# In the first attention, VectorE forms the difference of the two softmax maps and GpSimd normalises the head outputs

## The chip, the cores and the metric

The kernel runs on one core of one Trainium2 chip. The metric is the time of one launch in microseconds (us) on the device; the kernel before takes 1631.5 us, the median of three runs (1629.63 to 1633.35). Inside a core five engines run their own instruction queues and meet at semaphores: TensorE (PE, and PEld for its weight loads), VectorE (DVE), ScalarE (ACT), GpSimd (POOL) and SyncE (SP), which issues most transfers.

## The reference, cut to what matters

The program is two transformer blocks on a batch of 2 sequences of 1024 rows and 256 columns. The change lies in the attention of the first block, a differential attention: each of 8 heads has two causal softmax maps, and the second is subtracted with a factor.

```python
p1 = attn_map(q[:, :, :, 0], k[:, :, :, 0])
p2 = attn_map(q[:, :, :, 1], k[:, :, :, 1])
lam = lam1 - lam2 + LAMBDA_INIT
p = p1 - lam * p2
o = jnp.einsum('bhqk,bkhe->bqhe', p, v)
rms = jax.lax.rsqrt(jnp.mean(o * o, axis=-1, keepdims=True) + EPS)
o = o * rms * subln_w
o = o * (1.0 - LAMBDA_INIT)
return o.reshape(B, S, H * D) @ out_w.T + out_b
```

After it come a gated feed-forward layer with a Hadamard transform, a second attention with 16 small heads, and a feed-forward layer with a shared part and eight routed experts. None of these is touched.

## The kernel before, in words

**Groups and steps.** The 8 heads of the first attention are worked in 4 groups of 2 heads per sequence, `attn0_group(b, g, out, last)`. The heads of a group share their keys and values. A group has 16 steps: steps 0 to 7 are the eight query tiles (128 rows) of the first head, steps 8 to 15 those of the second. Step n has i + 1 key tiles of 128 columns for query tile i, so its width goes from 128 to 1024 columns in steps 0 to 7 and again in 8 to 15. In the last group of a sequence the second head takes its tiles in the order 0, 1, 2, 3, 5, 7, 6, 4. Groups 1 and 2 of a sequence are one loop on the device; groups 0 and 3 are written out.

**One step.** TensorE multiplies queries and keys into two PSUM tensors, one for each map (`scores`, three passes of split float32). VectorE takes each row's negated maximum (`nmax`, L1806). ScalarE takes the exponential into E1 and E2 with the row sums in `lsum` (L1407). VectorE takes the reciprocals `rsum` (L1772) and forms `mixc` (L1774), which is minus lambda times sum 1 over sum 2. GpSimd multiplies E2 with `mixc` (L2271) and adds E1 (L2274); so E1 holds the difference up to the factor 1 / sum 1. TensorE turns E1 (`transpose_p`, L916), ScalarE rounds the result to PT_h (L1389), VectorE keeps the rest in PT_l (L1781), TensorE multiplies with the values (`weigh_values`), and VectorE evicts to O with the factor `rsum` (L1786).

**Who waits for whom.** The work of several steps is laid in one another. In step s VectorE has, in this order: `mix(s - 1)`, `low(s - 2)` (PT_l), the two maxima of step s, the eviction of a value tile with its bias (L1810, steps 0 to 5), and `output(s - 3)`. ScalarE has `high(s - 2)` (PT_h), the two exponentials of step s, the rounding of value tiles to V_h (L1411, steps 0 to 5) and the sum of squares of an output tile (L1394). TensorE has `transpose_p(s - 2)`, `scores(s)`, `weigh_values(s - 3)`. There is one PSUM tensor for each map, so `scores(s)` of a map waits until the exponential of step s - 1 has read it (semaphore `exp_done`). E1 and E2 are double buffered.

**GpSimd beside it.** In its queue, behind the two instructions of each step, stand V_l (the low part of a value tile, L2250: two each in steps 0 and 1, one each in steps 2 to 5), the low part of the next group's weights Wa_l (one piece each in steps 8 to 11), and at the end of a group the scaling of Wo_raw (L2262) and Wo_l.

**The out product.** A group's outputs are normalised and multiplied with the output weights while the next group runs (`out` is true for groups 1 to 3). VectorE normalises tile t of both heads into `On[t % 2]` with the factors `orstd` (L1724, two instructions of 256 columns): tiles 0 and 1 in steps 2 and 3, tiles 2 to 7 behind the low parts of the turned tiles 1 to 6, in steps 8 to 11. TensorE turns `On` (L844) in steps 7 to 11, ScalarE and VectorE split it (L1365, L1731), TensorE multiplies, and VectorE adds to X (L1767). The last group of a sequence has nothing behind it; its outputs are normalised by VectorE (tiles 0 and 1) and GpSimd (tiles 2 to 7, L2308) in its tail. Under "tail" the text means what stands behind step 15 (`tail0`).

Of the kernel before, what the change touches and what calls it, by code (L numbers as in the profile page):

```python
# [30 lines left out]
ALU = mybir.AluOpType  # L31
AX = mybir.AxisListType

P = 128
B, T, HID = 2, 1024, 256
NT = T // P
# [12 lines left out]
UNITS0 = 12  # L49
SPLIT_STEPS = (8, 9, 10, 11)  # L50
STEPS0 = 2 * NT

# [42 lines left out]
def program(nc, d, ctx):  # L95
# [203 lines left out]
    mix_ready = sem("mix_ready")  # L299
    mix_scaled = sem("mix_scaled")  # L300
    p_ready = sem("p_ready")
# [1346 lines left out]
    def _(dve):  # L1648
# [70 lines left out]
        def out_normalise(it, g, t):  # L1719

            if t >= 2:
                dve.wait_ge(ot_ps, NT * it + t - 1)
            for h in range(2):
                ins = nc.vector.tensor_scalar(On[t % 2][:, h:h + 1, :], O[:, t, bass.ds(g % 2 * 2 + h, 1), :],  # L1724
                                              orstd[:, h * NT + t:h * NT + t + 1], None, ALU.mult)
            ins.then_inc(on_done, 1)
# [29 lines left out]
        def attn0_group(b, g, out, last):  # L1756
            it = b * GROUPS0 + g

            def project_out(s, late):
                for kind, t in out0(s, late) if out else ():  # L1760
                    if kind == "t":
                        out_low(it - 1, t)
                        if 1 <= t < NT - 1:
                            out_normalise(it - 1, g + 1, t + 1)
                    else:
# [4 lines left out]
            def mix(n):  # L1770
# [4 lines left out]
                                               scalar=lsum[:, n % 4, 0:1], in1=neglam[:], op0=ALU.mult,  # L1775
                                               op1=ALU.mult).then_inc(mix_ready, 1)

            def low(n):
# [11 lines left out]
            for s in range(STEPS0):  # L1790
                if s >= 1:
                    mix(s - 1)
                if out and s in (2, 3):
                    if s == 2 and last:
                        dve.wait_ge(xb_done, 2 * b + 1)
                    elif s == 2:
                        dve.wait_ge(xd_in, 16 * b + 16)
                    out_normalise(it - 1, g + 1, s - 2)
                if s >= 2:
# [448 lines left out]
    def _(pool):  # L2248
# [14 lines left out]

        def attn0_group(b, g, last):
            it = b * GROUPS0 + g
            for n in range(STEPS0):
                w = (q_tile(n, last) + 1) * P
                e1, e2 = E1[n % 2][:, 0:w], E2[n % 2][:, 0:w]
                pool.wait_ge(mix_ready, STEPS0 * it + n + 1)
                pool.nop(nofuse=True)  # L2270
                nc.gpsimd.tensor_scalar(e2, e2, mixc[:, n % 4:n % 4 + 1], 1.0, ALU.mult,  # L2271
                                        ALU.mult).then_inc(mix_scaled, 1)
                pool.wait_ge(mix_scaled, STEPS0 * it + n + 1)
                nc.gpsimd.tensor_tensor(e1, e1, e2, ALU.add).then_inc(p_ready, 1)  # L2274
                for t in v_tiles(n):
                    pool.wait_ge(v_hi, NT * it + t + 1)
                    low(V_l[:, t, :].unsqueeze(1), O[:, t, bass.ds(g % 2 * 2 + 1, 1), :],
                        V_h[:, t, :].unsqueeze(1)).then_inc(v_lo, 1)
                if n in SPLIT_STEPS:
                    split_wa(it + 1, SPLIT_STEPS.index(n))  # L2280
                if last and n == STEPS0 - 2:
                    scale_wo(it)
# [14 lines left out]

        def out_normalise(b, t):

# [12 lines left out]
        def attn0_out(b):  # L2312
            for t in range(2, NT):
                out_normalise(b, t)
            ffn_split(b, 0)
# [29 lines left out]
        for b in range(B):  # L2345
            attn0_group(b, 0, False)
            with pool.Fori(1, GROUPS0 - 1) as g:
                attn0_group(b, g, False)
            if b == 0:
                pool.wait_ge(const_in, CONSTS * 16)  # L2350
            pool.wait_ge(y_added, 3 * NT * b + (GROUPS0 - 2) * NT)
            add_bias(0)
            attn0_group(b, GROUPS0 - 1, True)
            attn0_out(b)
# [127 lines left out]
```

## Time and profile before

| | before |
|---|---|
| time, median of three runs | 1631.5 us |
| span of the profiled execution | 1649.7 us |
| PE busy | 1550.0 us (94%) |
| DVE busy | 1101.0 us (67%) |
| ACT busy | 930.4 us (56%) |
| POOL busy | 636.6 us (39%) |
| one group of the first attention with an out product | 106.3 us |

The span is that of one execution under the profiler, from its first to its last instruction; the page gives no time outside the span. The span is 18.2 us above the median of the runs. The eight groups of the first attention lie from about 29 to 430 us (first sequence) and from about 844 to 1246 us (second). A row of the chain or of the waits names the instruction that waited, what it waited for, and for how long.

### The profile page before, as it was taken

How to read it: one execution, taken by the hardware profiler on the slowest of the kernel's cores; microseconds unless marked ns; L12 is line 12 of the kernel's file. 1: busy time of each engine (PE TensorE's matmuls, PEld its weight loads, DVE VectorE, ACT ScalarE, POOL GpSimd, SP SyncE). 2: the span in 40 equal slices, each digit the busy share in tenths (PEclk: the TensorE clock that was granted, in tenths of full speed). 3: DMA queues.
4: the chain of work that ended last, by engine and by line, in shares of the span. 5: the costliest groups of instructions: out<-in, count | busy, mean ns of one | idle time of the engine just before them, and what ended most of it. 6: DMA issues, size and time to landing. Idle time of an engine off the chain costs nothing.

```text
span 1649.7 us, 30985 instructions
## 1 busy us (share of the span) xinstructions
PE 1550.0 (94%) x10774; PEld 1341.8 (81%) x10774; DVE 1101.0 (67%) x2705; ACT 930.4 (56%) x2054; POOL 636.6 (39%) x582
## 2 busy tenths in 40 slices
PE   8999999999899999999898999999998999998985
PEld 7888889888888677688787898898988876776885
DVE  6767667677645787574577676676766377874655
ACT  5666565665444577543556655656654346775353
POOL 1635444554461101252535354444654510031631
PEclk9999999999999999999999999999999999999998
DMA  3110000020120422034220200000201113322132
GB/s 132 46 52 17 27 1 16 25 91 1 40 69 10 75 51 61 21 120 137 76 96 1 77 18 26 16 7 18 91 1 58 50 36 61 60 60 101 56 126 106
DMA packets 48195, 88.03 MB, mean 53 GB/s; under 512 B 9600, under 2 KB 30480, under 8 KB 46928
## 3 DMA queue, kind: packets, MB, share of 16 engines
q1 hardware_dynamic: 43552, 75.28, 15.9%
q0 software_dynamic: 3744, 10.26, 1.7%
q8 instruction: 77, 1.26, 0.3%
q10 hardware_dynamic: 768, 0.79, 0.2%
q14 instruction: 54, 0.44, 0.1%
HBM read 60.18 MB, written 19.76 MB: 48 GB/s over the span
## 4 chain that ended last, share of the span: by engine, by line
PE 66%; DVE 15%; ACT 9%; issue 6%; POOL 3%; ACTq 1%; DMA 0%; DVEq 0%; POOLq 0%; SPq 0%
PE ps L408 16%; PE ps L410 15%; PE ps L409 15%; PE ps L1193 4%; PE ps L1210 4%; PE ps L1153 4%; ACT E L1407 3%; DVE nmax L1806 3%; PE ps L916 2%; POOL E L2274 2%; ACT PT_h L1389 1%; DVE On L1724 1%; DVE PT_l L1781 1%; PE ps L1189 1%; PE ps L844 1%
## 5 line engine op out<-in xcount | busy, mean ns | idle before, releaser
L1407 ACT ACTIVATE E<-ps,nmax 128x128 f32<-128x128 f32 (+7 forms) x256 | 188.9, 741 | 208.5 <-DVE nmax L1806 208.2
L2271 POOL TENSOR_SCALAR E<-E,mixc 128x128 f32<-128x128 f32 (+7 forms) x128 | 97.0, 758 | 396.2 <-DVE mixc L1774 396.2
L1806 DVE TENSOR_REDUCE nmax<-ps 128x1 f32<-128x128 f32 (+7 forms) x256 | 183.3, 749 | 12.7 <-PE ps L893 12.5
L1568 ACT ACTIVATE PT<-ps 128x512 f32<-128x512 f32 x288 | 155.0, 601 | 58.8 <-PE ps L1193 57.7
L2274 POOL TENSOR_TENSOR E<-E 128x128 f32<-128x128 f32 (+7 forms) x128 | 182.4, 1425 | 10.7
L408 PE MATMUL ps<-V_h,PT_h 128*128 128x256 f32 x576 | 168.0, 292 | 0.5 <-DVE O L1786 0.5
L409 PE MATMUL ps<-V_l,PT_h 128*128 128x256 f32 x576 | 163.8, 284 | 0.0
L410 PE MATMUL ps<-V_h,PT_l 128*128 128x256 f32 x576 | 163.6, 284 | 0.0
L408 PE MATMUL ps<-K_h,Q_h 128*128 128x512 f32 (+3 forms) x384 | 147.4, 384 | 8.7 <-ACT E L1407 5.4
L2026 DVE CUSTOM_DVE_ANT_0 masked<-ps,causal 128x128 bf16<-128x128 f32 (+3 forms) x256 | 111.1, 487 | 39.5 <-PE ps L1153 37.8
L1781 DVE TENSOR_TENSOR PT_l<-ps,PT_h 128x128 fp32r<-128x128 f32 (+7 forms) x128 | 96.7, 756 | 60.7 <-ACT PT_h L1389 60.0
L410 PE MATMUL ps<-K_h,Q_l 128*128 128x512 f32 (+3 forms) x384 | 133.2, 347 | 0.0
L409 PE MATMUL ps<-K_l,Q_h 128*128 128x512 f32 (+3 forms) x384 | 132.7, 346 | 0.0
L1153 PE MATMUL ps<-KS,QS 128*128 128x512 f32 (+3 forms) x384 | 111.9, 371 | 3.3 <-issue 1.4
L408 PEld LDWEIGHTS ps<-V_h,PT_h 128*128 128x128 f32 x576 | 110.5, 192 | 2.2 <-issue 0.9
L1193 PE MATMUL ps<-QS,KS 128*128 128x512 f32 (+3 forms) x384 | 112.2, 361 | 0.0
L409 PEld LDWEIGHTS ps<-V_l,PT_h 128*128 128x128 f32 x576 | 110.8, 192 | 0.5
L410 PEld LDWEIGHTS ps<-V_h,PT_l 128*128 128x128 f32 x576 | 110.6, 192 | 0.0
L408 PE MATMUL ps<-XT_h,Fw_h 128*128 128x512 f32 x256 | 102.6, 401 | 5.9 <-DVE XT_l L1654 2.8
L1866 DVE TENSOR_TENSOR Hf<-ps,silu_g 128x512 f32<-128x512 f32 x64 | 44.2, 691 | 88.8 <-PE ps L410 74.0
L916 PE MATMUL ps<-ident,E 128*128 128x128 f32 x576 | 85.0, 275 | 19.1 <-POOL E L2274 18.8
L409 PE MATMUL ps<-XT_l,Fw_h 128*128 128x512 f32 x256 | 100.9, 394 | 1.1 <-issue 1.0
(265 smaller groups left out, 4622.8 us busy)
## 6 DMA issues: line engine op xcount, KB each, us to landing
Wa_raw<-in_wa SPq DMA_DIRECT2D x8, 1024.0 KB, 6.0
Fw_raw<-in_fa SPq DMA_DIRECT2D x32, 256.0 KB, 2.6
E_raw<-in_fe SPq DMA_DIRECT2D x8, 768.0 KB, 7.5
xs<-in_xs SPq DMA_DIRECT2D x2, 2967.0 KB, 12.6
Wo_raw<-in_wo SPq DMA_DIRECT2D x8, 512.0 KB, 3.5
yg<-ys SPq DMA_DIRECT2D x8, 512.0 KB, 5.2
xg<-xs SPq DMA_DIRECT2D x6, 645.0 KB, 8.1
KS<-QK_h SPq DMA_DIRECT2D x56, 64.0 KB
```

Of the source, the lines that this page charges most:

```text
L408: nc.tensor.matmul(out, a_h, b_h, start=start, stop=False, **kw)
L409: nc.tensor.matmul(out, a_h, b_l, start=False, stop=False, **kw)
L410: return nc.tensor.matmul(out, a_l, b_h, start=False, stop=stop, **kw)
L916: mm = nc.tensor.transpose(ps[2][:, tile(kb)], E1[n % 2][:, tile(kb)], ident[:])
L1153: mm = nc.tensor.matmul(bank1(j % RING1)[:, at:at + z - a], QS[:, 2 * (p % Q_PAIRS) + n, tile(i)], KS[:, p % K_PAIRS, a:z], start=at == 0, ...
L1193: mm = nc.tensor.matmul(bank[:, at:at + z - a], KS[:, p % K_PAIRS, tile(kb)], QS[:, 2 * (p % Q_PAIRS) + n, a:z], start=not diagonal and k ...
L1407: nc.scalar.activation(e[:, 0:w], ps[m][:, 0:w], ACT.Exp, bias=nmax[:, s % 4, m:m + 1], accum_out=lsum[:, s % 4, m:m + 1]).then_inc(exp_do ...
L1568: nc.scalar.activation(PT[:, at:at + HALF], bank1(RING1 + n % RING1), ACT.Exp, scale=SCALE1).then_inc(t_used, 1)
L1781: nc.vector.tensor_tensor(PT_l[n % 2][:, 0:w], ps[2][:, 0:w], PT_h[n % 2][:, 0:w].bitcast(F32), ALU.subtract).then_inc(pt_lo, 1)
L1806: nc.vector.tensor_reduce(nmax[:, s % 4, m:m + 1], ps[m][:, 0:(q_tile(s, last) + 1) * P], AX.X, ALU.max, negate=True).then_inc(nmax_ready[ ...
L2026: ins = nc.vector.tensor_tensor_reduce(out=masked[:, j % RING1, cols], in0=scores, in1=causal[:, HALF - (z - a):], scale=-1.0, scalar=3e38 ...
L2274: nc.gpsimd.tensor_tensor(e1, e1, e2, ALU.add).then_inc(p_ready, 1)
```

## The change

GpSimd's two instructions on E1 and E2 are gone. In their place VectorE has one SCALAR_TENSOR_TENSOR behind `mixc`: E1 becomes E2 times `mixc` plus E1. It waits for `mixc` by the semaphore `mix_ready`. In the other direction the normalising of the outputs in groups 1 to 3 goes from VectorE (two instructions of 256 columns a tile) to GpSimd (one TENSOR_TENSOR of 512 columns a tile, with the factor spread over 256 columns): tiles 0 and 1 at the head of the group, tile 2 in step 7, tiles 3 and 4 in step 8, 5 and 6 in step 9, 7 in step 10, ahead of the Wa_l pieces of these steps. GpSimd has a wait for `or_done` at the head of the group and for `ot_ps` ahead of tiles 2 to 7 (the turning of the tile two before has been done, so that the buffer is free). The tail of the last group keeps its instructions.

```diff
--- before.py
+++ after.py
@@ -48,6 +48,7 @@
 PROJ0 = 2 * D0 + 2 * 2 * D0 + E0
 UNITS0 = 12
 SPLIT_STEPS = (8, 9, 10, 11)
+ON_STEPS = {7: (2,), 8: (3, 4), 9: (5, 6), 10: (7,)}
 STEPS0 = 2 * NT
 
 
@@ -297,7 +298,6 @@
     exp_done = [sem("exp_done0"), sem("exp_done1")]
     rsum_ready = sem("rsum_ready")
     mix_ready = sem("mix_ready")
-    mix_scaled = sem("mix_scaled")
     p_ready = sem("p_ready")
     pt_ps = sem("pt_ps")
     pt_hi = sem("pt_hi")
@@ -1718,8 +1718,6 @@
 
         def out_normalise(it, g, t):
 
-            if t >= 2:
-                dve.wait_ge(ot_ps, NT * it + t - 1)
             for h in range(2):
                 ins = nc.vector.tensor_scalar(On[t % 2][:, h:h + 1, :], O[:, t, bass.ds(g % 2 * 2 + h, 1), :],
                                               orstd[:, h * NT + t:h * NT + t + 1], None, ALU.mult)
@@ -1760,8 +1758,6 @@
                 for kind, t in out0(s, late) if out else ():
                     if kind == "t":
                         out_low(it - 1, t)
-                        if 1 <= t < NT - 1:
-                            out_normalise(it - 1, g + 1, t + 1)
                     else:
                         dve.wait_ge(y_mm, NT * (it - 1) + t + 1)
                         nc.vector.tensor_tensor(X[:, t, 0:HID], ring[t % 2 * 2 + 1][:, 0:HID], X[:, t, 0:HID],
@@ -1774,6 +1770,11 @@
                 nc.vector.scalar_tensor_tensor(out=mixc[:, n % 4:n % 4 + 1], in0=rsum[:, n % 8, 1:2],
                                                scalar=lsum[:, n % 4, 0:1], in1=neglam[:], op0=ALU.mult,
                                                op1=ALU.mult).then_inc(mix_ready, 1)
+                w = (q_tile(n, last) + 1) * P
+                e1, e2 = E1[n % 2][:, 0:w], E2[n % 2][:, 0:w]
+                dve.wait_ge(mix_ready, STEPS0 * it + n + 1)
+                nc.vector.scalar_tensor_tensor(out=e1, in0=e2, scalar=mixc[:, n % 4:n % 4 + 1], in1=e1, op0=ALU.mult,
+                                               op1=ALU.add).then_inc(p_ready, 1)
 
             def low(n):
                 w = (q_tile(n, last) + 1) * P
@@ -1790,12 +1791,11 @@
             for s in range(STEPS0):
                 if s >= 1:
                     mix(s - 1)
-                if out and s in (2, 3):
-                    if s == 2 and last:
+                if out and s == 2:
+                    if last:
                         dve.wait_ge(xb_done, 2 * b + 1)
-                    elif s == 2:
+                    else:
                         dve.wait_ge(xd_in, 16 * b + 16)
-                    out_normalise(it - 1, g + 1, s - 2)
                 if s >= 2:
                     low(s - 2)
                 if s == NT:
@@ -2261,21 +2261,28 @@
                 w = Wo_raw[:].rearrange("p (h c) n -> p c h n", c=KC)[:, c]
                 nc.gpsimd.tensor_scalar(w, w, subln[:, c:c + 1], 1.0, ALU.mult, ALU.mult).then_inc(wo_scaled, 1)
 
-        def attn0_group(b, g, last):
+        def out_normalise(it, g, t):
+
+            if t >= 2:
+                pool.wait_ge(ot_ps, NT * it + t - 1)
+                pool.nop(nofuse=True)
+            scales = orstd[:].rearrange("p (h t) -> p h t", h=2)[:, :, t:t + 1].to_broadcast([P, 2, E0])
+            nc.gpsimd.tensor_tensor(On[t % 2][:], O[:, t, bass.ds(g % 2 * 2, 2), :], scales, ALU.mult).then_inc(on_done, 1)
+
+        def attn0_group(b, g, out, last):
             it = b * GROUPS0 + g
+            if out:
+                pool.wait_ge(or_done, 2 * it)
+                pool.nop(nofuse=True)
+                for t in range(2):
+                    out_normalise(it - 1, g + 1, t)
             for n in range(STEPS0):
-                w = (q_tile(n, last) + 1) * P
-                e1, e2 = E1[n % 2][:, 0:w], E2[n % 2][:, 0:w]
-                pool.wait_ge(mix_ready, STEPS0 * it + n + 1)
-                pool.nop(nofuse=True)
-                nc.gpsimd.tensor_scalar(e2, e2, mixc[:, n % 4:n % 4 + 1], 1.0, ALU.mult,
-                                        ALU.mult).then_inc(mix_scaled, 1)
-                pool.wait_ge(mix_scaled, STEPS0 * it + n + 1)
-                nc.gpsimd.tensor_tensor(e1, e1, e2, ALU.add).then_inc(p_ready, 1)
                 for t in v_tiles(n):
                     pool.wait_ge(v_hi, NT * it + t + 1)
                     low(V_l[:, t, :].unsqueeze(1), O[:, t, bass.ds(g % 2 * 2 + 1, 1), :],
                         V_h[:, t, :].unsqueeze(1)).then_inc(v_lo, 1)
+                for t in ON_STEPS.get(n, ()) if out else ():
+                    out_normalise(it - 1, g + 1, t)
                 if n in SPLIT_STEPS:
                     split_wa(it + 1, SPLIT_STEPS.index(n))
                 if last and n == STEPS0 - 2:
@@ -2295,7 +2302,7 @@
                 pool.wait_ge(fw_hi, (CHUNKS - FW_RING) * b + (c if c < CH_F0 else c - FW_RING) + 1)
             low(Fw_l[c % FW_RING][:], Fw_raw[c % 2][:], Fw_h[c % FW_RING][:]).then_inc(fw_lo, 1)
 
-        def out_normalise(b, t):
+        def last_normalise(b, t):
 
             it, g = b * GROUPS0 + GROUPS0 - 1, GROUPS0 - 1
             if t in (2, NT // 2):
@@ -2311,7 +2318,7 @@
 
         def attn0_out(b):
             for t in range(2, NT):
-                out_normalise(b, t)
+                last_normalise(b, t)
             ffn_split(b, 0)
 
         def add_bias(row):
@@ -2343,14 +2350,16 @@
         for free in (sq_done, wo_lo):
             pool.sem_inc(free, 1)
         for b in range(B):
-            attn0_group(b, 0, False)
+            attn0_group(b, 0, False, False)
+            if b == 0:
+                pool.wait_ge(rows_out, 80)
             with pool.Fori(1, GROUPS0 - 1) as g:
-                attn0_group(b, g, False)
+                attn0_group(b, g, True, False)
             if b == 0:
                 pool.wait_ge(const_in, CONSTS * 16)
             pool.wait_ge(y_added, 3 * NT * b + (GROUPS0 - 2) * NT)
             add_bias(0)
-            attn0_group(b, GROUPS0 - 1, True)
+            attn0_group(b, GROUPS0 - 1, True, True)
             attn0_out(b)
             ffn0(b)
             nc.gpsimd.memset(causal[:, 0:HALF - P], 0.0).then_inc(filled, 1)
```

VectorE, in a loop group, from the maxima of step 5 to those of step 7 (before). E1 and E2 are two buffers each, of 1024 columns; PT_l is the low part of the turned map, rsum and lsum are reciprocals and sums of rows.

```order
L1806 TENSOR_REDUCE nmax<-ps 128x1 x2
L1809 REGISTER_ALU
L1810 ISA
L1810 TENSOR_TENSOR O<-ps,bva 128x256
L1786 ISA
L1786 TENSOR_SCALAR O<-ps,rsum 128x256
L1772 RECIPROCAL rsum<-lsum 128x2
L1774 SCALAR_TENSOR_TENSOR mixc<-rsum,lsum,neglam 128x1
L1781 TENSOR_TENSOR PT_l<-ps,PT_h 128x640
L1805 REGISTER_ALU
L1806 TENSOR_REDUCE nmax<-ps 128x1 x2
```

VectorE at the same place now (the map's instruction names E by its buffer number).

```order
L1806 TENSOR_REDUCE nmax<-ps 128x1 x2
L1809 REGISTER_ALU
L1810 ISA
L1810 TENSOR_TENSOR O<-ps,bva 128x256
L1787 ISA
L1787 TENSOR_SCALAR O<-ps,rsum 128x256
L1768 RECIPROCAL rsum<-lsum 128x2
L1770 SCALAR_TENSOR_TENSOR mixc<-rsum,lsum,neglam 128x1
L1776 SCALAR_TENSOR_TENSOR E_1<-E_1,mixc 128x768
L1782 TENSOR_TENSOR PT_l<-ps,PT_h 128x640
L1805 REGISTER_ALU
L1806 TENSOR_REDUCE nmax<-ps 128x1 x2
```

The map's instruction of step 5 (768 columns) stands between `mixc` and PT_l of step 4, and so ahead of the maxima of the next step.

GpSimd, in a loop group, steps 3 to 5 before:

```order
L2271 TENSOR_SCALAR E_1<-E_1,mixc 128x512
L2274 TENSOR_TENSOR E_1<-E_1 128x512
L2276 REGISTER_ALU
L2250 ISA
L2250 TENSOR_TENSOR V_l<-O,V_h 128x256
L2269 REGISTER_ALU
L2271 TENSOR_SCALAR E_0<-E_0,mixc 128x640
L2274 TENSOR_TENSOR E_0<-E_0 128x640
L2276 REGISTER_ALU
L2250 ISA
L2250 TENSOR_TENSOR V_l<-O,V_h 128x256
```

GpSimd from step 3 to step 8 now:

```order
L2250 TENSOR_TENSOR V_l<-O,V_h 128x256
L2281 REGISTER_ALU
L2250 ISA
L2250 TENSOR_TENSOR V_l<-O,V_h 128x256
L2281 REGISTER_ALU
L2250 ISA
L2250 TENSOR_TENSOR V_l<-O,V_h 128x256
L2267 ISA
L2270 ISA
L2270 TENSOR_TENSOR On<-O,orstd 128x512
L2267 REGISTER_ALU
L2270 ISA
```

V_l no longer stands behind a map; it starts as soon as ScalarE has written V_h of its tile. Behind the last V_l comes `On` of tile 2.

## Rows read from the trace of the kernel before

**Rows 1.** The page: the span, and the busy times of the engines.
```profile
span 1649.7 us, 30985 instructions
PE 1550.0 (94%) x10774; PEld 1341.8 (81%) x10774; DVE 1101.0 (67%) x2705; ACT 930.4 (56%) x2054; POOL 636.6 (39%) x582
```

**Rows 2.** Waits of the whole span: who, for whom; us, times, longest.
```profile
DVE PT_l L1781 <- ACT PT_h L1389: 60.0, 84, 2.5
...
PE ps L916 <- POOL E L2274: 18.8, 34, 2.1
...
PE ps L844 <- DVE On L1724: 9.4, 8, 2.9
```

**Rows 3.** Timeline of ScalarE, step 7 of a group: start, duration, instruction, idle before.
```profile
255.01 1.01 ACT L1407 ACTIVATE E<-ps,nmax 128x896 f32<-128x896 f32 x1
...
256.41 0.79 ACT L1389 CAST PT_h<-ps 128x768 fp32r<-128x768 f32 x1
259.36 1.11 ACT L1407 ACTIVATE E<-ps,nmax 128x1024 f32<-128x1024 f32 x1 [2.16 <-DVE nmax L1806]
```

**Rows 4.** Timeline of VectorE, the same step.
```profile
256.35 0.22 DVE L1774 SCALAR_TENSOR_TENSOR mixc<-rsum,lsum,neglam 128x1 f32<-128x1 f32 x1
257.23 0.96 DVE L1781 TENSOR_TENSOR PT_l<-ps,PT_h 128x768 fp32r<-128x768 f32 x1 [0.67 <-ACT PT_h L1389]
258.11 2.35 DVE L1806 TENSOR_REDUCE nmax<-ps 128x1 f32<-128x1024 f32 x2
```

**Rows 5.** Timeline of GpSimd and of TensorE, the same step.
```profile
256.74 1.01 POOL L2271 TENSOR_SCALAR E<-E,mixc 128x896 f32<-128x896 f32 x1 [1.66 <-DVE mixc L1774]
257.83 2.12 POOL L2274 TENSOR_TENSOR E<-E 128x896 f32<-128x896 f32 x1
...
255.50 0.48 PE L408 MATMUL ps<-K_h,Q_h 128*128 128x512 f32 x1
```

**Rows 6.** One line each: duration ns least/median/largest, first and last start.
```profile
L1704 DVE SCALAR_TENSOR_TENSOR Q_l<-ps,ba,Q_h x64: 741/751/753, 17.7 to 1151.7; 128x512 fp32r<-128x512 f32 x64
...
L1921 DVE SCALAR_TENSOR_TENSOR X<-yg,share,X x32: 453/480/919, 836.5 to 1641.1; 128x256 f32<-128x256 f32 x32
...
L2250 POOL TENSOR_TENSOR V_l<-O,V_h x64: 724/737/749, 31.6 to 1175.2; 128x256 fp32r<-128x256 f32 x64
```

**Rows 7.** Groups of VectorE, 232 to 262 us: busy, mean ns | idle before.
```profile
L1781 DVE TENSOR_TENSOR PT_l<-ps,PT_h 128x128 fp32r<-128x128 f32 (+5 forms) x6 | 3.7, 622 | 2.3 <-ACT PT_h L1389 2.3
...
L1724 DVE TENSOR_SCALAR On<-O,orstd 128x256 f32 x4 | 1.5, 403 | 0.0
```

**Rows 8.** Groups of VectorE, 292 to 311.5 us (steps 12 to 15).
```profile
L1806 DVE TENSOR_REDUCE nmax<-ps 128x1 f32<-128x640 f32 (+3 forms) x8 | 7.9, 1017 | 0.9 <-PE ps L893 0.9
L1781 DVE TENSOR_TENSOR PT_l<-ps,PT_h 128x384 fp32r<-128x384 f32 (+3 forms) x4 | 3.0, 758 | 1.8 <-ACT PT_h L1389 1.7
```

**Rows 9.** Timeline: ends of V_h and of mixc in step 3; Wo_l behind Wo_h.
```profile
238.93 0.40 ACT L1411 CAST V_h<-O 128x256 fp32r x1
...
239.27 0.22 DVE L1774 SCALAR_TENSOR_TENSOR mixc<-rsum,lsum,neglam 128x1 f32<-128x1 f32 x1
...
214.26 1.05 ACT L1443 CAST Wo_h<-Wo_raw 128x1024 fp32r<-128x1024 f32 x1
...
215.40 2.40 POOL L2250 TENSOR_TENSOR Wo_l<-Wo_raw,Wo_h 128x1024 fp32r<-128x1024 f32 x1 [4.53 <-ACT Wo_h L1443]
```

**Rows 10.** Timeline: VectorE's mixc while GpSimd works on E.
```profile
877.67 0.94 DVE L1774 SCALAR_TENSOR_TENSOR mixc<-rsum,lsum,neglam 128x1 f32<-128x1 f32 x1
...
876.25 2.35 POOL L2274 TENSOR_TENSOR E<-E 128x1024 f32<-128x1024 f32 x1
```

**Rows 11.** Groups of GpSimd by shape: the TENSOR_TENSOR of 512 columns.
```profile
L2274 POOL TENSOR_TENSOR E<-E 128x512 f32<-128x512 f32 x16 | 20.6, 1284 | 1.3
```

**Rows 12.** TensorE's waits, 846 to 922 us (group 0 of the second sequence).
```profile
PE ps L916 <- POOL E L2274: 6.1, 8, 2.1
```

**Rows 13.** TensorE's waits, 192 to 298 us (106 us of two loop groups).
```profile
PE ps L844 <- DVE On L1724: 0.6, 1, 0.6
```

## The prediction

> **What bounds the kernel now.** I read the page's busy times first: TensorE is busy for 94% of the span, VectorE for 67%, GpSimd for 39% [rows 1]. So what a wait costs counts by what it does to TensorE. Then the waits: TensorE stands before the turning of a map until GpSimd has formed it, 18.8 us in all over 34 of 128 steps, and before the turning of `On` for VectorE, 9.4 us over 8 times [rows 2]. These are what the change can win. Last the timeline of one wide step, to see whether VectorE can take the work, for VectorE's average of 67% does not tell that.
>
> In step 7 of a loop group the exponential of the second map of step 6 ends at 256.02; ScalarE rounds PT_h to 257.20; VectorE takes PT_l from 257.23 and the maxima from 258.11, and the next exponential starts at 259.36, having waited 2.16 us for the maximum [rows 3, 4]. That is a closed ring: exponential, PT_h, PT_l, maxima, exponential. TensorE is hardly in it: it began the scores of step 7 at 255.50, about 0.4 us after the first map's exponential had left PSUM at about 255.1 [rows 3, 5]. So in the wide steps two things run level, TensorE's work and the ring over VectorE and ScalarE. `mixc` ends at 256.57 and VectorE then idles 0.67 us for PT_h [rows 4]. GpSimd's pair lies outside the ring: it ends at 259.95, 3.4 us behind `mixc` [rows 4, 5]. The new instruction lies inside it, ahead of PT_l and of both maxima.
>
> **The cost of the new instruction.** The trace has the same operation at 256 columns with both streams in SBUF, 0.480 us, and at 512 columns with one in PSUM, 0.751 us [rows 6]. The slope is 0.271 us for 256 columns, or 1.06 ns a column, with 0.21 us beneath. That gives 0.35, 0.48, 0.62, 0.75, 0.88, 1.02, 1.15 and 1.29 us for the eight widths, 6.54 us a head, and 105 us for the 16 heads. The largest of the line, 0.919 us, is the upper end of the 256-column price.
>
> **Steps 0 to 7 of a group with an out product.** Between 232 and 262 us VectorE would run the maps of steps 0 to 6: 5.25 us. Out of that come its idle time before PT_l, 2.3 us, and the four `On` instructions, 1.5 us [rows 7]. 1.45 us are left, and they stand in the ring, so the ring is that much longer. VectorE's other idle times there are waits for the exponential, part of the ring itself.
>
> **The collision with V_l.** In four of these steps (2 to 5) GpSimd runs one V_l of 0.737 us [rows 6], now as soon as V_h is written. V_h of step 2 ends at 239.33; GpSimd's Wo_l followed its Wo_h (end 215.31) after 0.09 us; so V_l would start at about 239.42 to 239.5. `mixc` ends at 239.49, and the new instruction can't start before about 239.52 [rows 9]. V_l is first, by a hair. What that costs is seen elsewhere: `mixc` itself, one column wide, took 0.94 us from 877.67 to 878.61, and GpSimd's TENSOR_TENSOR on E ended at 878.60 [rows 10]. A VectorE instruction that reads two tensors of SBUF stood until GpSimd was done. So the new one would wait 0.74 - 0.1 = 0.64 us in each of four steps, 2.5 us a group. From below: nothing, if VectorE comes first. I take the 2.5, since the order of the two starts speaks for it, and keep 0 for the range.
>
> The Trainium skill (SBUF — State Buffer, Who interferes with whom) states this as a rule that speaks against the change: a VectorE instruction with two SBUF inputs and a GpSimd instruction that reads SBUF share a port, and the second to issue "fully blocks" until the first is done. By that rule the sum has the 2.5 us in it, or has them on GpSimd's side if VectorE issues first; by a view that the engines do not meet it has none. The row on `mixc` agrees with it.
>
> **Steps 8 to 11.** TensorE has the out product here, maps are narrow (except that of step 7), and VectorE loses 12 `On` instructions. It is TensorE's stretch, so VectorE's gain hides behind it; what goes is TensorE's wait for `On`, 0.6 us a group [rows 13]. I take -0.5. The Wa_l pieces and `On` on GpSimd may hold up VectorE's maps as V_l does, but TensorE has its products in front of it; I cost that at nothing. If that cover were gone it would be up to four times the 1.28 us of such an instruction [rows 11], 5 us a group; I give it no share of its own.
>
> **Normalising on GpSimd.** Eight instructions of 512 columns at 1.284 us [rows 11], 10.3 us a group on an engine that loses its pairs. Tiles 0 and 1 are done at the head of the group; tile t needs the turning of tile t - 2, which lies a product or more ahead of its own turning. No one waits for it: 0. The wait for `or_done` has only V_l behind it, and the second `or_done` comes before the group begins.
>
> **Steps 12 to 15.** The maps of steps 12 to 14, 0.88 + 1.02 + 1.15 = 3.05 us, go ahead of PT_l in steps 13 to 15, against 1.7 us of waits for PT_h [rows 8]: +1.35. The one before it (0.75 us, in step 12) meets VectorE's 0.9 us of waiting for TensorE's scores [rows 8] and costs nothing. The map of step 15 falls into the tail, where TensorE has projections to do: 0.
>
> **What TensorE keeps off.** The ring starts with about 0.4 us of lead over TensorE [rows 3, 5], in either half of the group: -0.8.
>
> One group with an out product: 1.45 + 2.5 - 0.5 + 1.35 - 0.8 = 4.0 us. There are six: 24 us.
>
> **Groups 0.** Here VectorE has more to do and is late with `mixc`, and TensorE waits longest for GpSimd: 6.1 us in that of the second sequence [rows 12]. The maps of steps 2 to 6 (4.4 us) lengthen VectorE's queue there, and no `On` goes out. But the map is ready at once, and the first turning behind them loses its wait of 2.1 us [rows 12]. The later ones give some 3 us more, against 1.35 us in steps 13 to 15. I take +1 us for each of the two groups; the bounds are -5 and +5.
>
> **The sum.** 24 + 2 = 26 us on the profiled execution, whose span is 1649.7 us [rows 1], 18.2 us over the median of the runs. Carried over by the ratio 1631.5 / 1649.7 it is 25.7 us: **1657 us**.
>
> **The rivals.**
> - *No collision* (VectorE's map starts before V_l, or the two don't meet): the 2.5 us go, a group costs 1.5 us, and the sum is 9 + 2 = 11 us: 1642 us. For it: the starts lie within 0.1 us of each other [rows 9]. Against it: where VectorE comes late to `mixc`, V_l is running already.
> - *The map's latency decides* (faster): TensorE waits for GpSimd's map and not for the ring. The place is the turning of a map, where the ready time moves from 3.4 us behind `mixc` to 1.3. Then all of the 18.8 us and 9.4 us [rows 2] could go, at most 28 us; half of it is likelier, since behind a wait stands the next: 1631 - 14 = 1617 us. It decides if TensorE's idle time goes while the maximum of the next step does not come later. For it: 34 waits are in the trace. Against it: 60.0 us of VectorE's idle time before PT_l over 84 times [rows 2] is 0.71 us each, less than a wide map.
> - *It cancels* (within 0.2%, which is 3 us and about what a measurement of this kernel can tell from no change): no collision, and group 0 gives back its waits, 9 - 10 = -1 us: 1631 us.
> - *Collisions everywhere*: V_l twice in steps 0 and 1, and Wa_l and `On` holding up VectorE until TensorE waits too, 2 us a group more: 1657 + 14 = 1671 us.
>
> **How the numbers follow.** Forecast 0.45 (its own range 1649 to 1665), no collision 0.25, latency 0.15, cancelling 0.07, collisions everywhere 0.08. Faster holds the latency case and a little of the cancelling one: 0.17. The same: 0.07. Slower: 0.76. The range leaves out most of the latency case and the far end of the last: 1627 to 1668.
>
> **What would show it.** TensorE's wait for the map (18.8 us) is near nothing, and in its place stand waits of the scores for the exponential (L408 for L1407), some 0.5 us a wide step. VectorE's busy time goes up by 105 us less 96 `On` instructions of 0.40 us [rows 7], so about 66 us, plus its waits inside instructions. A map of 384 to 768 columns in steps 2 to 5 lasts some 0.6 us longer than the same width in steps 10 to 13. VectorE's idle time before PT_l is gone in wide steps. A loop group takes about 4 us longer (106.3 us before). The forecast is wrong if the maps in steps 2 to 5 have their bare price, or if a group takes no longer than before; then the ring was not closed where I put it, and the maximum had slack.

## The result, and the profile after

The changed kernel takes 1669.3 us (1668.5 to 1670.7 over 4 runs) against 1631.5 us: a ratio of 1.0226, 95% interval 1.0214 to 1.0239. It is slower, as forecast, but by 37.8 us and not by 25.7, and it lies 1.3 us above the upper end of the range.

The page of the kernel after: the span, the busy times, and the group of the new instruction.

```profile
span 1668.9 us, 30665 instructions
...
PE 1554.7 (93%) x10774; PEld 1341.5 (80%) x10774; DVE 1191.0 (71%) x2737; ACT 929.4 (56%) x2054; POOL 419.5 (25%) x374
...
L1776 DVE SCALAR_TENSOR_TENSOR E<-E,mixc 128x128 f32<-128x128 f32 (+7 forms) x128 | 125.8, 983 | 4.5
```

The 128 new instructions are busy for 125.8 us where the bare prices gave 105. For the rest a word on the baseline: the profiled execution of before had a span of 1649.7 us [rows 1], and the same program profiled again (`before2`, below) has this page:

```profile
span 1629.0 us, 30985 instructions
...
PE 1544.4 (95%) x10774; PEld 1340.3 (82%) x10774; DVE 1101.4 (68%) x2705; ACT 932.0 (57%) x2054; POOL 637.5 (39%) x582
```

Of the 20.7 us between them 1.6 lie in group 0 of the second sequence, where TensorE's granted clock was 0.90 in steps 7 to 11 (1.00 in `before2`), and the rest outside the first attention. From here on "before" is this second profile; the kernel after has a span 39.9 us longer.

TensorE's waits, whole span, kernel after (who, for whom: us, times, longest):

```profile
PE ps L408 <- ACT E L1407: 30.1, 55, 1.3
PE ps L916 <- DVE O L1810: 7.7, 8, 1.0
PE ps L916 <- DVE PT_l L1782: 6.8, 12, 1.2
```

The wait for GpSimd's map [rows 2] is gone; the scores wait for the exponential instead (30.1 us, where before they did so for 5.4). VectorE's group of PT_l, whose idle time was 60.0 us in [rows 2], now has:

```profile
L1782 DVE TENSOR_TENSOR PT_l<-ps,PT_h 128x128 fp32r<-128x128 f32 (+7 forms) x128 | 96.0, 750 | 15.1 <-ACT PT_h L1389 14.7
```

VectorE's timeline of steps 6 and 7 of a loop group, kernel after; the second half answers to [rows 4]:

```profile
265.25 0.22 DVE L1770 SCALAR_TENSOR_TENSOR mixc<-rsum,lsum,neglam 128x1 f32<-128x1 f32 x1
265.51 1.53 DVE L1776 SCALAR_TENSOR_TENSOR E<-E,mixc 128x768 f32<-128x768 f32 x1
266.96 0.81 DVE L1782 TENSOR_TENSOR PT_l<-ps,PT_h 128x640 fp32r<-128x640 f32 x1
267.70 2.07 DVE L1806 TENSOR_REDUCE nmax<-ps 128x1 f32<-128x896 f32 x2
...
271.39 1.15 DVE L1776 SCALAR_TENSOR_TENSOR E<-E,mixc 128x896 f32<-128x896 f32 x1
272.46 0.95 DVE L1782 TENSOR_TENSOR PT_l<-ps,PT_h 128x768 fp32r<-128x768 f32 x1
273.33 2.35 DVE L1806 TENSOR_REDUCE nmax<-ps 128x1 f32<-128x1024 f32 x2
```

Map, PT_l and maxima stand back to back. The map of 896 columns has its forecast price of 1.15 us; that of 768, one step earlier, takes 1.53 us. GpSimd's timeline beside it, and the same width in the second half of the group, where no V_l is left:

```profile
265.49 0.74 POOL L2250 TENSOR_TENSOR V_l<-O,V_h 128x256 fp32r<-128x256 f32 x1 [4.53 <-ACT V_h L1411]
```

```profile
316.98 1.02 DVE L1776 SCALAR_TENSOR_TENSOR E<-E,mixc 128x768 f32<-128x768 f32 x1
```

V_l starts 0.02 us before the map, which takes 0.51 us longer. The map ends at 267.04, which is 0.81 us behind the end of V_l at 266.23. That is the price of its 768 columns without the fixed 0.21 us, as if the map had moved no column until V_l was done, while its fixed part passed. In steps 2 to 5 that happens once each, and in step 1 two V_l hold up `mixc` (0.75 us for 0.22) and the map (0.93 for 0.48), 0.98 us together. All in all 3.0 us a group.

How far the group goes by stretch, between the starts of VectorE's reciprocal of steps 0, 7, 11 and 15, in us (out group: the third of the first sequence; group 0: the whole, in each sequence):

| kernel | 0 to 7 | 7 to 11 | 11 to 15 | tail | out group | groups 0 |
|---|---|---|---|---|---|---|
| before | 28.8 | 30.0 | 19.4 | 28.0 | 106.2 | 96.9, 96.2 |
| after | 32.6 | 29.6 | 21.0 | 27.7 | 110.9 | 103.3, 102.1 |
| maps_only | 33.7 | 32.8 | 21.2 | 27.7 | 115.3 | 103.3, 102.1 |
| on_only | 28.4 | 36.3 | 19.4 | 27.9 | 112.1 | 96.9, 96.3 |
| vl_behind | 29.7 | 32.9 | 20.6 | 27.7 | 110.9 | 100.6, 99.7 |
| group0_pair | 32.6 | 29.6 | 20.9 | 27.7 | 110.8 | 96.8, 96.0 |
| vl_wait | 29.6 | 29.6 | 21.0 | 27.7 | 107.9 | 101.8, 100.3 |
| map_late | 31.2 | 29.2 | 21.2 | 29.3 | 110.9 | 103.2, 102.5 |
| map_1col | 29.7 | 29.2 | 19.4 | 27.8 | 106.1 | 98.7, 95.8 |
| narrow | 28.7 | 29.6 | 19.4 | 27.9 | 105.7 | 99.1, 98.1 |
| on_ahead | 28.4 | 28.6 | 19.4 | 27.9 | 104.4 | 96.9, 96.3 |

The six out groups are 4.4 to 4.9 us longer each (the last of a sequence counted up to step 15), 27.8 us in all, and the two groups 0 are 6.5 and 5.9 us longer. The sum is 40.1 us, and the spans differ by 39.9: nothing of weight happens elsewhere. The medians of the runs differ by less, 37.8 us, since the profiled execution of the kernel after was the slowest of its four (1670.7 us).

### The profile page after: what moved, and what is told of

It is laid out like the page before. It is cut to its first block, busy times and chain, and to the rows that moved or that the text cites. A ratio compares the mean times of both kernels' runs of the same rounds, so it can differ in the third digit from the quotient of the medians.

```text
span 1668.9 us, 30665 instructions
## 1 busy us (share of the span) xinstructions
PE 1554.7 (93%) x10774; PEld 1341.5 (80%) x10774; DVE 1191.0 (71%) x2737; ACT 929.4 (56%) x2054; POOL 419.5 (25%) x374
## 4 chain that ended last, share of the span: by engine, by line
PE 60%; DVE 23%; ACT 8%; issue 6%; POOL 1%; ACTq 1%; DMA 1%; DVEq 0%; SPq 0%
PE ps L408 14%; PE ps L410 13%; PE ps L409 13%; DVE nmax L1806 5%; ACT E L1407 5%; PE ps L1193 4%; PE ps L1210 4%; PE ps L1153 4%; DVE E L1776 4%; DVE PT_l L1782 3%; DVE mixc L1770 1%; PE ps L844 1%; PE ps L1189 1%; POOL xs L2396 1%; PE ps L916 1%
## 5 line engine op out<-in xcount | busy, mean ns | idle before, releaser
L2026 DVE CUSTOM_DVE_ANT_0 masked<-ps,causal 128x128 bf16<-128x128 f32 (+3 forms) x256 | 110.9, 486 | 39.4 <-PE ps L1153 37.9
L1776 DVE SCALAR_TENSOR_TENSOR E<-E,mixc 128x128 f32<-128x128 f32 (+7 forms) x128 | 125.8, 983 | 4.5
L408 PEld LDWEIGHTS ps<-K_h,Q_h 128*128 128x128 f32 x384 | 72.1, 188 | 59.8 <-ACT E L1407 46.1
L408 PE MATMUL ps<-XT_h,Fw_h 128*128 128x512 f32 x256 | 102.5, 400 | 5.1 <-DVE XT_l L1654 2.7
L1782 DVE TENSOR_TENSOR PT_l<-ps,PT_h 128x128 fp32r<-128x128 f32 (+7 forms) x128 | 96.0, 750 | 15.1 <-ACT PT_h L1389 14.7
L410 PE MATMUL ps<-XT_h,Fw_l 128*128 128x512 f32 x256 | 101.3, 396 | 0.0
```

The source lines that it names most:

```text
L408: nc.tensor.matmul(out, a_h, b_h, start=start, stop=False, **kw)
L410: return nc.tensor.matmul(out, a_l, b_h, start=False, stop=stop, **kw)
L1776: nc.vector.scalar_tensor_tensor(out=e1, in0=e2, scalar=mixc[:, n % 4:n % 4 + 1], in1=e1, op0=ALU.mult, op1=ALU.add).then_inc(p_ready, 1)
L1782: nc.vector.tensor_tensor(PT_l[n % 2][:, 0:w], ps[2][:, 0:w], PT_h[n % 2][:, 0:w].bitcast(F32), ALU.subtract).then_inc(pt_lo, 1)
L2026: ins = nc.vector.tensor_tensor_reduce(out=masked[:, j % RING1, cols], in0=scores, in1=causal[:, HALF - (z - a):], scale=-1.0, scalar=3e38 ...
```

## The experiments

Ratios are to the kernel before, with 95% intervals. Edits are to the changed kernel unless said.

**maps_only**: the kernel before, with only the map moved to VectorE.

```diff
 # VectorE, behind mixc
+ nc.vector.scalar_tensor_tensor(out=e1, in0=e2, scalar=mixc[...], in1=e1, op0=ALU.mult, op1=ALU.add)
 # GpSimd
- nc.gpsimd.tensor_scalar(e2, e2, mixc[...], 1.0, ALU.mult, ALU.mult)
- nc.gpsimd.tensor_tensor(e1, e1, e2, ALU.add)
```

> Half of the change: VectorE forms the maps, the normalising stays on VectorE as before. Theory (the map stands in the ring exponential, PT_h, PT_l, maxima, exponential): slower than the changed kernel, since the On instructions of steps 2 and 3 (1.5 us) and TensorE's wait for On (0.5 us) come back in six groups: 1669 + 12 = 1681 us, a loop group 112 to 113 us. Rival (what costs is the normalising on GpSimd, or its waits): at most 1645 us.

1695.1 us, 1.0384 (1.0363 to 1.0405): slower than the whole change by 26 us. With `On` left on VectorE, steps 7 to 11 take 32.8 us for 29.6. TensorE's waits:

```profile
PE ps L408 <- ACT E L1407: 27.9, 47, 1.3
...
PE ps L408 <- DVE OT_l L1731: 12.2, 8, 1.9
```

So both the expected price of the map and, by more than expected, the help that GpSimd's normalising gives it are there. Groups 0 are as in the kernel after: they have no `On` of their own. A small part of the 26 us may be TensorE's clock: it fell to 1.2 GHz (granted 0.5) for 3.4 us eight times in the groups with an out product, and never there in the kernel after. The last groups of a sequence, without such a fall in steps 7 to 15, lose 4.1 us against the kernel after, where the others lose 4.5.

**on_only**: only `On` moves; the pair is back on GpSimd, ahead of V_l and `On`.

```diff
- VectorE's instruction behind mixc
 # GpSimd
 for n in range(STEPS0):
+    pool.wait_ge(mix_ready, STEPS0 * it + n + 1)
+    nc.gpsimd.tensor_scalar(...); nc.gpsimd.tensor_tensor(e1, e1, e2, ALU.add)
     for t in v_tiles(n): ...
     for t in ON_STEPS.get(n, ()) if out else (): ...
```

> The other half: GpSimd keeps its pair on E1 and E2 and takes the normalising as well. Theory (the ring without the map, TensorE's wait for On gone): 0.5 to 1.5 us less a group with an out product, 1622 to 1629 us, faster than before. Rival (GpSimd's normalising holds up what stands behind it): 1640 us or more.

1666.0 us, 1.0208 (1.0191 to 1.0225). The time is in the rival's range, but it is not what stands behind the normalising that is late. TensorE's waits, then GpSimd's timeline:

```profile
PE ps L845 <- POOL On L2266: 33.1, 24, 2.0
PE ps L917 <- POOL E L2283: 17.9, 29, 2.1
```

```profile
285.13 0.48 POOL L2280 TENSOR_SCALAR E<-E,mixc 128x256 f32<-128x256 f32 x1 [5.24 <-DVE mixc L1771]
285.69 0.72 POOL L2283 TENSOR_TENSOR E<-E 128x256 f32<-128x256 f32 x1
286.37 2.05 POOL L2266 TENSOR_TENSOR On<-O,orstd 128x512 f32<-128x512 f32 x2
```

GpSimd stood 5.24 us for `mixc`, with two `On` behind it that TensorE wanted. TensorE's waits for `On` are 33.1 us, 28.1 more than the 5.0 of before. The rest of the 34 us goes with TensorE's clock. In five of the six out groups it fell to 1.2 GHz (granted 0.5) for 3.4 us in steps 7 to 11, each time 0.6 to 1.5 us behind the end of a wait for `On` of 1.97 us. The sixth, the last of the second sequence, had as much waiting for `On` (5.5 us) and no such fall. Steps 7 to 11 of the third group and of that one, PE alone (stretch, us, busy, granted clock):

```profile
267.40:303.70 36.30, 30.75 (x236) 0.95 0.00 0
1198.00:1232.80 34.80, 29.23 (x235) 1.00 0.01 2
```

That is 1.5 us a group, some 7 us of the 34. Both parts come from the place in GpSimd's queue and not from the engine; `on_ahead`, below, moves only the place.

**vl_behind** and **vl_wait**: GpSimd's V_l waits until the step's map is formed; `vl_behind` puts Wa_l and `On` behind that wait too.

```diff
 for n in range(STEPS0):
+    if n < 6 or n in SPLIT_STEPS:   # vl_wait: if n < 6
+        pool.wait_ge(p_ready, STEPS0 * it + n + 1)
     for t in v_tiles(n): ...
```

> The changed kernel, but GpSimd waits for the map of the step (p_ready) ahead of V_l in steps 0 to 5 and ahead of On and Wa_l in steps 8 to 11, so that it doesn't read SBUF while VectorE forms the map. Theory with the collision: maps have the bare price at every step (0.62 us for 384 columns in step 2, where the changed kernel has 1.12), the maps' busy time falls from 125.8 to 105 us, and the time by some 15 us, to 1654 us. Rival (the long maps are long for another reason, or V_l late holds up TensorE): 1669 us or more.

1665.8 us, 1.0204 (1.0184 to 1.0224). Steps 0 to 7 gain 3.0 us a group, as expected, and steps 7 to 11 lose 3.3 us: TensorE waits for `On` again, by the mechanism of `on_only` (us, times, longest):

```profile
PE ps L844 <- POOL On L2270: 21.8, 18, 1.4
```

> The changed kernel with one wait more: GpSimd starts V_l of steps 0 to 5 only when VectorE has formed the map of the step; On and Wa_l keep their place and have no such wait (in the run vl_behind On stood behind the wait and cost 3.3 us a group in steps 7 to 11, while steps 0 to 7 gained 3.0). Theory: steps 0 to 7 of a loop group 29.7 us (32.6 in the changed kernel), the rest unchanged; 1669 - 6 x 2.9 - 5 = 1647 us. Rival (the late V_l pushes something else that vl_behind hid): 1655 us or more.

1650.5 us, 1.0109 (1.0093 to 1.0124): 18.8 us come back. VectorE's and GpSimd's timelines of the step that was shown:

```profile
258.91 1.02 DVE L1776 SCALAR_TENSOR_TENSOR E<-E,mixc 128x768 f32<-128x768 f32 x1
```

```profile
260.23 0.74 POOL L2250 TENSOR_TENSOR V_l<-O,V_h 128x256 fp32r<-128x256 f32 x1 [4.15 <-DVE E L1776]
```

The map has its bare price, V_l comes later, and TensorE has no wait for it. ScalarE's timeline gives the turn of the ring around this map, first of the kernel after and then of `vl_wait`:

```profile
263.14 0.90 ACT L1407 ACTIVATE E<-ps,nmax 128x768 f32<-128x768 f32 x1 [2.21 <-DVE nmax L1806]
...
268.81 1.01 ACT L1407 ACTIVATE E<-ps,nmax 128x896 f32<-128x896 f32 x1 [2.50 <-DVE nmax L1806]
```

```profile
256.55 0.90 ACT L1407 ACTIVATE E<-ps,nmax 128x768 f32<-128x768 f32 x1 [1.69 <-DVE nmax L1806]
...
261.70 1.01 ACT L1407 ACTIVATE E<-ps,nmax 128x896 f32<-128x896 f32 x1 [1.98 <-DVE nmax L1806]
```

5.67 us against 5.15: what goes from inside the map (0.51 us) goes from the ring. The span of `vl_wait` (1648.8 us) is still 19.8 us over before, and that isn't the collision with V_l: the six out groups are 1.7 to 2.5 us longer each, 12.0 in all, the groups 0 make 9.0, and outside the eight groups 1.2 us come back. The 3.5 us missing to the expected 1647 are there too: the last group of each sequence gave back 1.9 to 2.0 us and not 2.9, and the groups 0 gave back 3.3 for the 5 expected.

**group0_pair**: the groups 0 keep GpSimd's pair.

```diff
- VectorE's instruction, always
+ if out:      # VectorE
+ if not out:  # GpSimd's pair
```

> The changed kernel, but the first group of each sequence has GpSimd's pair on E1 and E2 as before. Theory (group 0 loses as much as the others, which the prediction had at 1 us each): its 6.4 and 4.3 us come back, 1669 - 11 = 1658 us. Rival (the loss in group 0 comes with the profile or with something other than the map): 1667 to 1669 us.

1658.2 us, 1.0158 (1.0138 to 1.0177): 11.1 us come back, and the groups 0 alone change (96.8 and 96.0 us, as before).

**map_late**: the map of step s - 1 is formed behind the maxima of step s.

```diff
  # step s: PT_l, both maxima
+ if s >= 1: mapped(s - 1)     # and mapped(STEPS0 - 1) after the last mix
```

> The changed kernel with VectorE's map behind the two maxima of the next step, not ahead of PT_l. It no longer delays the maxima, and V_l has run by then. Theory of the ring (latency): it is faster than the changed kernel by what the map puts into the ring and the collisions, 3 to 5 us a group, 1635 to 1648 us, with new waits of TensorE for the map of up to 0.8 us in wide steps. Rival (VectorE is simply full in the wide steps, so that the place in its queue doesn't matter): 1650 us or more, and VectorE without idle time in steps 4 to 7.

1676.9 us, 1.0277 (1.0261 to 1.0293), and not by either mechanism. The waits of TensorE and VectorE, then VectorE's timeline:

```profile
DVE PT_l L1784 <- ACT PT_h L1389: 63.6, 77, 2.0
...
PE ps L916 <- DVE E L1778: 59.4, 76, 2.4
```

```profile
270.26 0.96 DVE L1784 TENSOR_TENSOR PT_l<-ps,PT_h 128x768 fp32r<-128x768 f32 x1 [1.14 <-ACT PT_h L1389]
271.13 2.47 DVE L1808 TENSOR_REDUCE nmax<-ps 128x1 f32<-128x1024 f32 x2
273.52 1.58 DVE L1778 SCALAR_TENSOR_TENSOR E<-E,mixc 128x896 f32<-128x896 f32 x1
```

VectorE has idle time again (63.6 us), and TensorE waits 59.4 us for the map. As I read these waits, the map's work behind the maxima is out of one ring but its latency is in another: map, turning, PT_h, PT_l, maxima, map. No run tests that ring by itself. In both places that were tried the map costs on VectorE's queue.

**map_1col**: the map has one column; the second softmax map is left out of the other columns.

```diff
- e1, e2 = E1[n % 2][:, 0:w], E2[n % 2][:, 0:w]
+ e1, e2 = E1[n % 2][:, 0:1], E2[n % 2][:, 0:1]
```

> The changed kernel with VectorE's map cut to one column (the rest of the second map is left out of the result): every wait and every instruction stays, 128 x 0.22 us in place of 105 us of maps and 21 us of waiting inside them. Theory (the columns of the map in the ring cost the time, not the handing over): steps 0 to 7 of a loop group at or under the 28.8 us of before, and the time under 1622 us, since no one waits for GpSimd's pair. Rival (the wait for mixc and the instruction's fixed part cost as much as the columns): 1635 us or more.

1631.4 us, 0.9992 (0.9983 to 1.0001), between the two. Steps 0 to 7 take 29.7 us: of the 3.9 us that the change adds there, 2.9 are the columns; the other 0.9 us are what the seven instructions cost with hardly any columns, collisions and all, net of what `On` gives back by leaving VectorE. VectorE's timeline, in a step with V_l and in one without:

```profile
147.68 0.73 DVE L1776 SCALAR_TENSOR_TENSOR E<-E,mixc 128x1 f32<-128x1 f32 x1
...
152.95 0.22 DVE L1776 SCALAR_TENSOR_TENSOR E<-E,mixc 128x1 f32<-128x1 f32 x1
```

```profile
147.66 0.74 POOL L2250 TENSOR_TENSOR V_l<-O,V_h 128x256 fp32r<-128x256 f32 x1 [3.94 <-ACT V_h L1411]
```

**on_ahead**: GpSimd's pair, as in `on_only`, but `On` ahead of it.

```diff
 for n in range(STEPS0):
+    for t in ON_STEPS.get(n, ()) if out else (): ...
+    pool.wait_ge(mix_ready, ...); nc.gpsimd.tensor_scalar(...); nc.gpsimd.tensor_tensor(...)
     for t in v_tiles(n): ...
-    for t in ON_STEPS.get(n, ()) if out else (): ...
```

> GpSimd keeps the pair and normalises, as in on_only, but On of a step stands ahead of the pair of that step in GpSimd's queue, not behind it. Theory of the queue (on_only lost 6.3 us in steps 7 to 11 of each group because On(3), On(5) and On(7) stood behind a pair that waits for mixc): the stretch is back at 29.5 to 30 us and the time at 1624 to 1630 us, faster than before. Rival (GpSimd is too slow for both, 1.28 us an On among pairs): 1640 us or more.

1621.7 us, 0.9933 (0.9920 to 0.9947): 10.7 us faster than before, which on this chip took 1632.5, and the fastest here but for `vl_spread`, which can't be told from it. GpSimd's timeline and TensorE's waits:

```profile
270.65 1.05 POOL L2266 TENSOR_TENSOR On<-O,orstd 128x512 f32<-128x512 f32 x1
...
273.99 1.04 POOL L2266 TENSOR_TENSOR On<-O,orstd 128x512 f32<-128x512 f32 x1 [2.29 <-PE ps L845]
...
276.15 0.48 POOL L2282 TENSOR_SCALAR E<-E,mixc 128x256 f32<-128x256 f32 x1 [1.12 <-DVE mixc L1771]
```

```profile
PE ps L917 <- POOL E L2285: 17.8, 29, 2.1
```

`On` runs while `mixc` is still to come. No wait for `On` is left among TensorE's largest, and the wait for the map is nearly as large as before (17.8 us for 18.8): the gain comes almost without touching it.

**narrow**: as `on_ahead`, with maps of up to 384 columns on VectorE and V_l of steps 0 to 2 behind them.

```diff
+ VectorE's instruction if q_tile(n, last) < 3, behind a wait for the map of step n - 1; GpSimd's pair otherwise
+ if n < 3: pool.wait_ge(p_ready, STEPS0 * it + n + 1)    # ahead of V_l
```

> Maps of up to three key tiles are formed by VectorE (0.35 to 0.62 us, in the place of the On instructions that leave it), wider ones by GpSimd's pair; On on GpSimd ahead of the pair, V_l of steps 0 to 2 behind VectorE's map. Theory: the narrow maps are out of the wide ring, TensorE's waits for GpSimd in steps 1, 2, 9 and 10 go; 1622 to 1628 us, faster than before. Rival (any map on VectorE costs): 1632 us or more.

1633.9 us, 1.0017 (1.0008 to 1.0027): 12 us slower than `on_ahead`. The rival was right: even the cheapest maps cost. The added wait for the map before is not what costs, for VectorE is never idle ahead of such a map. TensorE's waits:

```profile
PE ps L409 <- ACT E L1408: 13.0, 30, 1.0
PE ps L917 <- POOL E L2294: 12.4, 19, 2.1
```

There are 5.4 us less of waiting for the map than in `on_ahead`. In their place 13.0 us are spent waiting for the exponential, where `on_ahead` has 5.0, and 6.3 us for OT_l, the low part of the turned `On`, where it has 0.8.

**vl_spread**: `on_ahead` with the V_l tiles spread over steps 0 to 6.

```diff
- for t in v_tiles(n):
+ for t in ((0,), (1,), (2, 3), (4,), (5,), (6,), (7,))[n] if n < 7 else ():
```

> As on_ahead (GpSimd keeps the pair, On ahead of it), and V_l of tile 1 stands behind the pair of step 1, tiles 2 and 3 behind that of step 2, and so on, one step later than before. Theory: TensorE's wait for the map of step 1 (0.31 to 0.46 us in seven groups) goes, up to 3 us in all, 1619 to 1622 us. Rival (the next wait stands right behind, that for the exponential): the same as on_ahead, 1621.7 us, within 1.5 us.

1620.8 us, 0.9927 (0.9914 to 0.9941): no difference from `on_ahead` that these runs can tell, and its stretches agree with that kernel's within 0.3 us.

**before2**: the kernel before, unchanged.

> The kernel before, profiled again. The first profile's span is 1649.7 us where the runs took 1631.5 us; in it the stretch from step 15 of the fourth group to step 0 of the fifth took 426.1 us, in the changed kernel and its variants 411.5 to 413.3 us. Theory (one slow execution was profiled, the loss lies outside the first attention): span 1630 us, that stretch 412 to 414 us, a loop group 106.2 us as before. Rival (the kernel before always takes 426 us there, and the changed one gained 13 us outside the attention): 426 us again.

1630.8 us, one run, with the span of 1629.0 us shown above. From step 15 of the fourth group to step 0 of the fifth it takes 413.2 us where the first profile took 426.1: 13 of the 20.7 us are there, 6.0 behind step 15 of the last group, 1.6 in group 0 of the second sequence, and none in the out groups. Why the first profile was slower in the first two of these places stays open.

## Why the forecast had the sign and not the size

Step by step, measured against predicted, in us:

| term | predicted | measured |
|---|---|---|
| out group, steps 0 to 7 | 1.45 + 2.5 - 0.4 = 3.55 | 3.85 |
| steps 7 to 11 | -0.5 | -0.5 |
| steps 11 to 15 | 1.35 - 0.4 = 0.95 | 1.5 |
| tail | 0 | -0.2 |
| six out groups | 24 | 27.8 |
| both groups 0 | 2 | 12.3 |
| sum | 26 | 40.1 |

**The ring** was where I put it: PT_l's idle time fell from 60.0 us to 15.1, the exponential is what TensorE waits for, and the bare prices (0.35 to 1.29 us) hold to 0.01 us. VectorE's busy time rose by 89.6 us: the forecast 66, and the waits inside instructions.

`vl_wait`, where the collisions of steps 0 to 7 are gone, leaves 0.8 us there for the 1.45 - 0.4 = 1.05 of the forecast.

**The collision with V_l** is shown by `vl_wait`. I had taken 0.64 us in four steps, 2.5 us; it is 0.51 us in four and 0.98 us in step 1, which I had left to a rival: 3.0 us. The 0.64 was too much because the fixed part of the instruction passes during the wait, as [rows 10] already had it: `mixc` ended 0.01 us behind GpSimd, and not its own 0.22 us behind. The 3.0 was near 2.5 by luck: the price too high, the places too few. Of the other 0.5 us in steps 11 to 15, 0.3 are the same thing with another partner. The map of 512 columns at step 11 took 1.16 us beside GpSimd's scaling of Wo, which I had costed at nothing; in `vl_behind` GpSimd waits in that step too, the map takes 0.75 us, and the stretch 20.6 us for 21.0. The remaining 0.2 us have no cause shown.

The Trainium skill (SBUF — State Buffer, Who interferes with whom) has the rule that VectorE's second port into SBUF is shared with GpSimd, that it is an exclusive lock, and that the order of issue decides who is blocked. The runs agree: a map of 768 columns that started second ended 0.81 us behind V_l, all of its columns' time, and one of a single column ended 0.01 us behind it (0.73 us for 0.22). Only 0.51 of V_l's remaining 0.72 us show in the duration, because the fixed 0.21 us run meanwhile. It holds the other way round too: `On` starting 0.13 us behind the map of 1024 columns took 2.06 us for 1.04, and no one waited for it.

**Groups 0 is the step that failed**: 12.3 us for 2, which is 10.3 of the 14.1 us between 26 and 40.1 (the out groups have the other 3.8). I credited the change with TensorE's waits for GpSimd's map, 2.1 us at the first turning and some 3 us at the later ones. Those waits did go. TensorE's waits in group 0 of the first sequence, before and then after:

```profile
PE ps L916 <- POOL E L2274: 4.4, 6, 1.3
PE ps L408 <- ACT E L1407: 1.3, 3, 0.7
```

```profile
PE ps L408 <- ACT E L1407: 6.8, 10, 1.1
PE ps L916 <- DVE PT_l L1782: 2.5, 4, 1.2
PE ps L916 <- DVE O L1810: 1.0, 1, 1.0
PE ps L408 <- DVE O L1787: 0.7, 1, 0.7
```

4.4 us went, and 5.5 + 2.5 + 1.0 + 0.7 = 9.7 us came: the rest of VectorE's longer queue. This is what I had written of the latency rival, "behind a wait stands the next", and then did not apply to group 0. The credit should have been nothing. Without it, and with no `On` leaving VectorE there, group 0 costs by the prediction's own prices an out group's 4.0, plus the 1.5 that `On` gave there and the 0.5 of steps 8 to 11: 6.0 us each, 12 for both, against 12.3 measured. This was worked out afterwards, and only the sum comes out: steps 0 to 7 cost 4.5 and 3.6 us in the two groups where these prices give 5.05, and steps 7 to 11 cost 1.7 and 1.8 us where they give nothing. So that the credit was wrong is shown, and how the 12.3 us divide is not. `group0_pair` confirms the place: 11.1 us come back there and nowhere else.

**Normalising on GpSimd** was rightly costed at no wait, but at 1.284 us where it took 1.04 us. I gave it no worth of its own beyond 1.5 + 0.5 us a group. In `on_ahead` it is worth 1.8 us a group with the pair on GpSimd, and with the map on VectorE 115.3 - 110.9 = 4.5 us: the more VectorE has in the ring, the more an instruction taken out of it is worth. So the parts don't add up: +63 us and +34 us alone, +38 us together.

**Rivals.** No collision is out. Latency decides is out: `on_ahead` keeps 17.8 us of that wait and is the faster. Cancelling is out with both of its conditions: there was a collision, and group 0 gave nothing back. Collisions everywhere came nearest in time (1671), but that is luck: of the 2 us a group that it added only about 1 was found (0.98 us in step 1, 0.3 us at step 11), steps 7 to 11 cost no more than forecast, and the missing time was in groups 0. Scaling by 1631.5 / 1649.7 moved the sum by 0.3 us only.

**Open**: in `vl_wait` the map of 1024 columns in the last group of a sequence took 2.17 us though it started 0.05 us before an `On`, and ended 1.08 us behind it, so it had stood for the whole of `On`. In the kernel after, the same two with the same 0.05 us between their starts went the other way: the map took 1.28 us and `On` 2.14. Who goes first when both start so close, these runs don't settle.

## What to carry to other kernels

A wait that a change removes is a gain only up to the next wait behind it; where the work goes to an engine that is in a closed ring, count the credit as nothing. Price an instruction where its ring closes, and not by the engine's mean busy share: 1.15 us on VectorE cost more than 3.4 us on GpSimd outside the ring. And an engine with spare time is only as good as its queue's order: the same eight instructions a group cost 34 us behind a late wait, and gained 10.7 us ahead of it.

## What the runs showed of the hardware

A GpSimd instruction on SBUF that starts 0.02 us ahead makes a VectorE instruction with two SBUF inputs 0.51 us longer at 1, 384, 512, 640 and 768 columns alike, where the GpSimd instruction itself lasts 0.74 us. The VectorE instruction then ends behind the GpSimd one by its columns at about 1.05 ns each (0.81 us for 768 columns, 0.01 us for one). Started the other way round, GpSimd's instruction is held up: `On` of 1.04 us took 2.06 us beside a map of 1.28 us. A GpSimd TENSOR_TENSOR of 512 columns whose second operand is a scale spread over the columns takes 1.04 us, against 1.28 us with two full streams [rows 11].
